# Three passes of a membrane scan, looped or written out one by one, on one Trainium2 core

## What is computed

```python
mem = DECAY * mem + dt
hard = (mem > THR).astype(mem.dtype)
spike = sg + jax.lax.stop_gradient(hard - sg)
mem = mem - spike * THR
```

## Time and profile before

| | |
|---|---|
| median of 3 runs | 1695.24 us (1692.81 to 1695.54) |
| profiled execution: its time | 1701.06 us |
| profiled execution: span from first to last instruction | 1699.3 us |
| mean granted TensorE clock | 0.795 |
| busy: TensorE | 1178.4 us |
| busy: VectorE | 1103.5 us |
| busy: ScalarE | 601.2 us |
| busy: GpSimd | 198.3 us |

### The profile page before, as it was taken

How to read it: one execution, slowest core, us unless ns; L and a number is a source line. 1 busy time by engine, 2 the same in 40 slices (tenths; PEclk the granted TensorE clock), 3 DMA queues, 4 the chain that set the end, 5 groups by cost and what they waited for, 6 DMA issues and landing times. The chain is left out here.

```text
span 1699.3 us, 25028 instructions
## 1 busy us (share of the span) xinstructions
PE 1178.4 (69%) x8364; PEld 902.6 (53%) x8364; DVE 1103.5 (65%) x3471; ACT 601.2 (35%) x935; POOL 198.3 (12%) x189
## 2 busy tenths in 40 slices
PE   1230001488888988898888988889666879688786
PEld 1110001377777877787777876779423526346272
DVE  4788988777887778877797777872133325343251
ACT  3120000333444334443444534441325355363422
POOL 2000001301211012110211102110010102001000
PEclk8575555688899889898988999895578788886966
DMA  2000000000000000000000000000200000000000
GB/s 72 0 1 1 1 1 1 1 1 0 0 0 0 0 0 0 0 0 0 0 0 0 0 0 0 0 1 1 58 0 1 0 0 8 0 7 1 0 8 6
DMA packets 9746, 7.22 MB, mean 4 GB/s; under 512 B 3158, under 2 KB 7831, under 8 KB 9690
## 3 DMA queue, kind: packets, MB, share of 16 engines
q1 hardware_dynamic: 8170, 5.07, 1.1%
q10 hardware_dynamic: 1520, 1.48, 0.3%
HBM read 5.50 MB, written 1.05 MB: 4 GB/s over the span
## 5 line engine op out<-in xcount | busy, mean ns | idle before, releaser
L1133 DVE TENSOR_TENSOR delta_tm<-delta_tm,ps 128x256 f32<-128x256 f32 x96 | 40.4, 421 | 156.7 <-PE ps L836 156.7
L795 PE MATMUL ps<-delta_kq_up,delta_arena 64*128 64x128 f32 x1024 | 111.2, 400 | 37.2 <-ACT delta_kq L547 36.5
L795 PEld LDWEIGHTS ps<-delta_kq_up,delta_arena 64*128 64x128 f32 x1024 | 102.4, 302 | 62.2 <-ACT delta_kq L547 37.4
L893 PE MATMUL ps<-ones,beta_b 1*128 1x1 f32 x8 | 1.8, 346 | 190.9 <-PEq L339 190.9
L633 ACT ACTIVATE delta_xf<-ps 128x256 f32<-128x256 f32 (+1 forms) x128 | 48.9, 382 | 204.5 <-PE ps L823 140.2
L517 POOL TENSOR_TENSOR delta_km<-delta_beta_k,delta_arena 128x512 f32<-128x512 f32 x16 | 32.6, 2037 | 635.9 <-DVE delta_beta_k L1030 635.9
L834 PE MATMUL ps<-delta_xf,delta_tt 128*128 128x64 f32 x768 | 106.6, 284 | 0.0
L836 PE MATMUL ps<-delta_tt,delta_xf 128*128 128x64 f32 x768 | 106.6, 284 | 0.0
L823 PEld LDWEIGHTS ps<-delta_tm,drive 128*128 128x128 f32 x768 | 95.6, 201 | 17.0 <-DVE delta_zb L984 9.1
L893 PEld LDWEIGHTS ps<-ones,beta_b 1*128 1x128 f32 x8 | 1.8, 322 | 191.1 <-issue 191.1
L823 PE MATMUL ps<-delta_tm,drive 128*128 128x64 f32 x768 | 98.5, 284 | 6.1 <-ACT delta_tm L623 6.1
(11 more groups left out here) (372 smaller groups left out, 2923.1 us busy)
## 6 DMA issues: line engine op xcount, KB each, us to landing
out<-post_rows SPq DMA_DIRECT2D x4, 256.0 KB, 2.3
setup_wmod<-in_L_wmod ACTq DMA_DIRECT2D x2, 384.0 KB, 3.4
post_wff<-in_L_attn_Wff SPq DMA_DIRECT2D x3, 256.0 KB
post_w<-in_L_ffn_w SPq DMA_DIRECT2D x2, 256.0 KB
post_fc_q<-in_L_ffn_fc_q SPq DMA_DIRECT2D x2, 256.0 KB
setup_wspike<-in_L_attn_Wspike ACTq DMA_DIRECT2D x1, 256.0 KB
wq<-in_L_attn_Wq ACTq DMA_DIRECT2D x1, 256.0 KB
wk<-in_L_attn_Wk SPq DMA_DIRECT2D x1, 256.0 KB
```

The costliest lines, as they stand in the source:

```text
L795: ins = eng.matmul(m.ps[:, at + h % 2, P * (h // 2):P * (h // 2) + P], up_lift[s][ks, cs], m.kq_up[s][ks, :, half], start=True, stop=True)
L1133: eng.tensor_tensor(v, v, m.ps[:, 6 + n, 0:256].rearrange("p (b s) -> p b s", s=s), ALU.subtract).then_inc(vector_back, vec.one(f"TX{x}{s}"))
```

## The change

The loop over the three sure passes becomes a Python loop, so that the program holds three copies of the pass, one behind the other:

```diff
-            with eng.Fori(0, SURE) as _:
+            for _ in range(SURE):
                 a_pass()
             with eng.If(changed() > 0):
                 with eng.Fori(0, NT - SURE) as _:
```

## The result

The change makes the kernel faster by 0.6%: the median is 1684.16 us (6 runs, 1682.55 to 1686.61) beside 1695.23 us of the kernel before, a ratio of 0.9941 with a 95% interval of 0.9928 to 0.9954. The forecast was 1684.6 us. The profiled execution took 1682.55 us, its span 1680.8.

A forecast was written before the change was run, and what follows sets the result against it. VectorE alone was taken to bound the membrane stage, the only one changed. Jumps back -10.5, counter's instructions -0.3 and block boundaries +0.2 summed to -10.6 us, taking the 1695.24 us median to 1684.6, range 1681 to 1690.

The forecast's parts named there:

- The two jumps back: Membrane stage, VectorE's gaps between passes: 5.62 + 5.57 us become 0.35 us each, saving 10.5 us (9.0 to 11.0).
- Two fetches, one for the jump and one for the block's end: Each gap between passes holds two code reads: some 2.8 us behind the branch, some 2.4 between second and third clear.
- The counter's instructions: Loop's register move at the start, arithmetic and untaken branch after pass three: they go, saving 0.1 + 0.2 = 0.3 us.
- the jump out: Skip over the unentered If after pass three: one code fetch, 2.7 us before and after, no change.
- Block boundaries: Code block ends in the membrane passes: one formerly hidden may now cost 0 to 0.4 us, taken as 0.2.
- the two places left open: Boundary 512 instructions after the first pass's: it meets line 387's wait (hidden) or the operation behind it (not hidden).
- The two small terms: The counter's instructions, 0.3 us saved, and the block boundaries, 0.2 us added.
- The count of instructions: VectorE's program grows by 1038 instructions, 8 x 128 + 14, so later code moves 14 places within a block.
- The loops behind it: Later loops, including the recurrence's of 197 VectorE instructions: still three blocks, no code fetched within it, no change.
- The slower rival: Recurrence's loop no longer stays in instruction memory: 15 jumps back at 2.8 us, 42 us, time 1726 us; chance 2%.
- The clock's rival: Recurrence stage: TensorE's granted clock of 0.87 falls, 1% costing some 8 us, leaving 1692.4 us; chance 5%.
- A sign that was not met: Membrane stage to end at about 279.7 us instead of 290.3, both later stages as long as before within 2 us.

The follow-up runs named there:

- the move by eight: The looped kernel before the change, with eight more semaphore clears at the very start of VectorE's program: 1690.8 us, ratio 0.9974.
- the move by 118: The looped kernel before the change, with 118 more semaphore clears at the very start of VectorE's program: 1696.4 us, one run.
- the loops of clears: The kernel after the change, with six three-round loops of 60 to 620 semaphore clears ahead of the first pass: 2240.5 us, one run.

## Why the prediction was right

- *The two jumps back*, 10.5 us: 5.62 + 5.57 became 0.32 + 0.31, so 10.56. The clears were priced right from the first pass's rows.
- *Two fetches, one for the jump and one for the block's end*: the move by eight took the second out of the way, the move by 118 put it behind nine step instructions. This was the reading on which the whole sum rested, and it holds.
- *The counter's instructions*, 0.3 us: the entry became 0.09 us shorter (1.10 to 1.01 us idle before the first step); at the way out only 0.03 is seen (5.57 to 5.54), as the jump out took 2.9 us instead of 2.8. So 0.12 and not 0.3.
- *Block boundaries*, +0.2 us: of the two places left open it was the one that costs nothing. The third clear is at 95.0, the first step at 95.49, so the boundary lies at the first step, and 512 instructions on it meets the wait of line 387. The end of pass one takes as long as that of pass two, 1.65 us from the last step's start to the next pass. The two small terms were both off and cancel (-0.3 + 0.2 forecast, -0.12 measured); that is luck.
- *The count of instructions*: the boundary moved by one place, from the third clear to the first step, and L404's register move at 95.7 is followed at once by the first clear, at 95.8. So the listing's jump into the loop takes no place in the program as it runs: it is 1039 instructions longer, not 1038, and the later code lies 15 places on, not 14. Nothing in the sum hangs on it.
- *What the sum lacked*: the stage fell by 11.2, not 10.6. 0.44 us of it are the steps, 175.94 us busy instead of 176.38. That is not the change's: the looped kernel moved by eight has 175.90 as well, so the execution profiled before was a little slow.
- *The loops behind it*: 914.9 us instead of 915.5, no packet from 400 to 1070 us. The slower rival is refuted as to its ground: a body of 300 instructions is held, and this one has 197. (Its price was reckoned with 15 jumps back; 15 rounds have 14.) The clock's rival didn't come: 0.88 beside 0.87 in the recurrence.
- *A sign that was not met*: the later stages were to stay as long within 2 us. Against the profile before, the last one is 5.8 us shorter and the stage's end comes at 277.8 us, not 279.7. The 5.8 us are in that profile's execution, which was 5.8 us over its median, and not in the medians.

That the median came within 0.4 us of the 1684.6 is closer than these runs can tell: its own six spread over 4.1 us, and against the kernel before beside it the gain was 11.1 us in one set and 10.3 in the next. What the experiments show is the mechanism and the 10.6 us of the gaps.

## What to carry to other kernels

The jump back of a loop on VectorE is nearly free, 0.2 to 0.4 us, as long as its body spans no more than three blocks of code (300 instructions here); a body that spans four or more (420 and up) stands still for a fetch in each round, and for two if its head lies at a block's end. Look for idle time that is as long at every round's start, put down to "remote" or "issue", with a packet of the instruction queue in it; then write the rounds out, shorten the body, or move the code by a few instructions where the engine waits anyway, and keep a conditional part short that is nearly always skipped, since jumping over a long one is the same fetch. Only VectorE's loops were varied here.

## What the runs showed of the hardware

- VectorE's code comes in packets of 8 KB (0.16 MB in 20 packets), each about 128 instructions: one per 14.4 us of steps at 112.6 ns, one per 11.0 us of clears at 86 ns.
- A taken jump to code held takes 0.2 to 0.4 us from the branch's start, to code that is not 2.7 to 3.0 us. The block behind it comes 2.4 to 2.9 us after the first, by the starts of the packets in the kernels before, moved by 8 and by 118. The packet itself is a small part: at the first jump it moves at 156.6 us, 1.0 behind the branch and 1.8 ahead of the first clear.
- Four blocks are held, the one read ahead among them: the loop of 300 clears ran two rounds without a packet, that of 420 read five per round. The jumps back took 0.3 and 2.8 us.
- The order of the fetches matters: in the move by 118 the engine ran nine step instructions and stopped within the straight code behind a jump.
- A block's end costs the sequencer time in straight code too, unseen while the engine has work queued. In the loops of clears, two clears across an end are 0.44 to 0.52 us apart where a block is read ahead and 0.18 to 0.21 where none is, against 0.08 to 0.09 elsewhere.
- A read-ahead in vain, whose packet had moved just before the branch, didn't delay the jump's own fetch: 2.8 us (move by 118, jump out).
